# A selective-scan layer with a mixture of experts: products of VectorE moved behind further scans, and the output tiles of one chunk spread over four tiles

## What is computed

```python
proj = xn @ W_in.T                      # x and gate, 1024 channels each
x = silu(conv_b + sum_j conv_w[:, j] * shifted(x, j))     # 4 taps
ts, Bm, Cm = rms parts of x @ W_x.T     # 32, 16 and 16 wide
dt = softplus(ts @ W_dt.T + b_dt)
state = state * exp(dt * A) + (dt * x) * B_t      # per token, 1024 x 16 states
y = sum over the states of state * C_t
s = ((y + x * D) * silu(gate)) @ W_out.T
```

## Time and profile before

| what | us |
|---|---|
| three runs | 1053.42, 1053.86, 1055.64 |
| median | 1053.86 |
| the profiled execution, its own time | 1055.66 |
| its span in the trace | 1053.8 |
| busy: VectorE, GpSimd, TensorE, ScalarE | 986.1, 905.0, 851.3, 727.2 |
| mean granted clock of TensorE, share of full speed | 0.916 |

### The profile page before, as it was taken

How to read it: one execution, slowest core, us unless ns; L and a number is a source line. 1 busy time by engine, 2 the same in 40 slices (tenths; PEclk the granted TensorE clock), 3 DMA queues, 4 the chain that set the end, 5 groups by cost and what they waited for, 6 DMA issues and landing times.

```text
span 1053.8 us, 10364 instructions
## 1 busy us (share of the span) xinstructions
PE 851.3 (81%) x2756; PEld 316.7 (30%) x2756; DVE 986.1 (94%) x1027; ACT 727.2 (69%) x1281; POOL 905.0 (86%) x320
## 2 busy tenths in 40 slices
PE   9944558989878998999756759999888998779468
PEld 6321113333323343333212213333323333223123
DVE  6779999999999999999999899999999988999996
ACT  3656766888877767888565566878778576667543
POOL 0616899979989998989898979799998988999996
PEclk9976669999989999999877879999999999889788
DMA  9947659887778577676843743966648566664735
GB/s 337 348 154 305 229 193 330 289 296 272 267 265 334 180 256 268 241 264 216 272 130 132 217 194 121 332 240 216 219 172 301 187 214 236 228 230 170 279 51 149
DMA packets 86585, 245.93 MB, mean 233 GB/s; under 512 B 9344, under 2 KB 10752, under 8 KB 79872
## 3 DMA queue, kind: packets, MB, share of 16 engines
q1 hardware_dynamic: 67712, 197.03, 52.3%
q10 hardware_dynamic: 12672, 31.46, 7.6%
q0 software_dynamic: 6144, 16.78, 6.1%
HBM read 183.11 MB, written 62.13 MB: 233 GB/s over the span
## 4 chain that ended last, share of the span: by engine, by line
POOL 27%; PE 24%; DVE 18%; issue 11%; DMA 10%; ACT 7%; SPq 2%; ACTq 0%; DVEq 0%; POOLq 0%
POOL drive L593 16%; DVE sc_ps L1197 7%; POOL drive L606 6%; PE x_ps L1519 5%; DMA rep<-rep_rows 5%; PE f_ps L1472 4%; DMA rep_rows<-dtu 3%; DVE drive L1197 3%; PE dt_ps L1447 3%; DVE drive L1207 3%; PE y_ps L1487 3%; ACT sc_ps L806 2%; PE x_ps L1383 2%; POOL slot_x L557 2%; POOL moe L578 2%
## 5 line engine op out<-in xcount | busy, mean ns | idle before, releaser
L593 POOL TENSOR_TENSOR drive<-rep,b_all 128x2048 f32<-128x2048 f32 x127 | 579.0, 4598 | 46.8 <-DMA rep<-rep_rows 37.5
L806 ACT ACTIVATE sc_ps<-rep,a_neg 128x512 f32<-128x512 f32 x512 | 331.2, 681 | 93.7 <-DVE drive L1207 68.1
L1487 PE MATMUL y_ps<-drive,stack 128*32 128x512 f32 x1024 | 152.2, 669 | 108.6 <-DVE drive L1207 68.1
L606 POOL TENSOR_TENSOR drive<-drive,c_all 128x1024 f32<-128x1024 f32 x92 | 219.7, 2388 | 10.1 <-ACT state L785 10.0
L1197 DVE TENSOR_TENSOR_SCAN sc_ps<-sc_ps,state,drive 128x512 f32<-128x512 f32 x164 | 202.4, 1272 | 2.1 <-POOL drive L593 1.4
L1207 DVE TENSOR_TENSOR drive<-sc_ps,c_all 128x1024 f32<-128x1024 f32 x164 | 199.8, 1219 | 3.5
L1197 DVE TENSOR_TENSOR_SCAN sc_ps<-sc_ps,drive 128x512 f32<-128x512 f32 x164 | 193.4, 1214 | 9.2 <-ACT sc_ps L806 5.2
L1472 PE MATMUL f_ps<-w_ring,xT_slot 128*128 128x512 f32 x368 | 172.8, 613 | 23.5 <-ACT xT_slot L816 22.4
L1447 PE MATMUL dt_ps<-xnT,w_g 128*128 128x512 f32 x232 | 120.5, 667 | 23.5 <-ACT dtu L773 23.5
L1197 DVE TENSOR_TENSOR_SCAN drive<-sc_ps,state,drive 128x512 f32<-128x512 f32 x92 | 113.8, 1268 | 7.7 <-ACT sc_ps L806 7.7
L1197 DVE TENSOR_TENSOR_SCAN drive<-sc_ps,drive 128x512 f32<-128x512 f32 x92 | 109.8, 1210 | 3.1 <-ACT sc_ps L806 2.0
(11 more groups left out here) (189 smaller groups left out, 1057.5 us busy)
## 6 DMA issues: line engine op xcount, KB each, us to landing
rep<-rep_rows SPq DMA_DIRECT2D x128, 512.0 KB, 6.1
w_ring<-wring SPq DMA_DIRECT2D x46, 1024.0 KB, 6.1
rep_rows<-dtu ACTq DMA_DIRECT2D x32, 512.0 KB, 2.7
x_slot<-slot_x SPq DMA_DIRECT2D x46, 256.0 KB, 7.0
slot_rows<-y_slot ACTq DMA_DIRECT2D x46, 256.0 KB, 4.3
w_g<-wg_in SPq DMA_DIRECT2D x32, 256.0 KB, 7.4
w_x<-wx_in SPq DMA_DIRECT2D x24, 256.0 KB, 5.2
slot_x<-zeros SPq DMA_DIRECT2D x1, 5888.0 KB, 20.5
```

Of the source, the lines that this page charges most:

```text
L593: pool.tensor_tensor(drive[:, m % RING, :, :], rep[:, n % 2, :, 1, :], b_all[:, q:q + 1, :].broadcast_to([P, NR, TC]), ALU.mult).then_inc( ...
L606: pool.tensor_tensor(drive[:, m % RING, 0:2, :], drive[:, m % RING, 0:2, :], c_all[:, q:q + 1, :].broadcast_to([P, 2, TC]), ALU.mult).then ...
L806: act.activation(sc[:, r, :], rep[:, n % 2, r, 0, :], ACT.Exp, scale=a_neg[:, lo:lo + 1]).then_inc(decay_ok, 1)
L1487: last = pe.matmul(y_ps[CH * r:CH * (r + 1), :], stack[:, :], drive[:, m % RING, r, :], start=False, stop=(m % NQ == NQ - 1))
```

## The change

Four things are changed; every computation stays the same.

- The low product, where VectorE has it, moves from behind scan 1 to behind scan 2 in quads 0, 2 and 3 of every tile (in quad 1, and in quad 3 of the last tile, it stays).
- In the tiles of `SILU_SOON`, the first scan of quad 2 moves ahead of the high product of quad 1, and the first scan of quad 3 ahead of the high product of quad 2.
- `SILU_SOON` loses tiles 0.7, 1.0, 1.1 and 2.7, and so holds 3.0 to 3.6.
- The output tiles of chunk 2 are spread over 3.0 to 3.3, one each, all in halves; for chunk 0 the split stays as it was. The second half goes behind the step sizes' matmul, its copy on ScalarE behind the softplus, and the copy of a whole output tile (chunk 0 only) behind the store of dt and u and `decays(m + 1, 0)`.

```diff
--- before.py
+++ after.py
@@ -52,7 +52,7 @@
 EARLY_X = {3: 1, 4: 3, 5: 5, 6: 7}
 STEPS_AMONG_SCANS = (1, 3, 5, 10, 15, 19, 21, 26, 27, 29)
 GATE_BEHIND = (3, 5, 9, 10, 15, 18, 19, 21, 25, 26, 27, 29, 30)
-SILU_SOON = (7, 8, 9, 23, 24, 25, 26, 27, 28, 29, 30)
+SILU_SOON = (24, 25, 26, 27, 28, 29, 30)
 LATE_X = {2: 0, 3: 2, 4: 4, 5: 6}
 
 
@@ -82,6 +82,18 @@
 
 def late_x(c, t):
     return LATE_X.get(t) if c < NCH - 1 else None
+
+
+def split_out(c, t):
+    if c % PER_ROW == 0:
+        return None
+    if c == NCH - 1:
+        return t if t < TT else None
+    return 2 * t if t < TT // 2 else None
+
+
+def whole_out(c, t):
+    return 2 * t + 1 if c % PER_ROW and c < NCH - 1 and t < TT // 2 else None
 
 
 def pool_pairs(m):
@@ -926,15 +938,14 @@
                 elif t < NT - 1:
                     keep_dt(n + 1)
                 copy_slot_y(b, left_slot)
-                if not even and t in (1, 2):
-                    copy_out(c - 1, 2 * t - 1)
                 diagonal(n)
                 if t < NT - 1:
                     keep_rows(n + 1)
                 store_slot(b, left_slot)
-                if not even and t in (1, 2):
-                    store_out(c - 1, 2 * t - 1)
                 decays(m + 1, 0)
+                if t and whole_out(c, t - 1) is not None:
+                    copy_out(c - 1, whole_out(c, t - 1))
+                    store_out(c - 1, whole_out(c, t - 1))
                 if chunk_end:
                     keep_dt(n + 1)
                     keep_rows(n + 1)
@@ -971,14 +982,13 @@
                 if rms_tile:
                     rms(c + 1)
                 decays(m + 3, 1)
-                if not even and t in (0, 1):
-                    copy_out(c - 1, 2 * t)
-                if not even and t in (0, 1):
-                    store_out(c - 1, 2 * t)
                 if rms_tile:
                     rms_root(c + 1)
                 elif n + 2 < TILES:
                     softplus(n + 2)
+                if split_out(c, t) is not None:
+                    copy_out(c - 1, split_out(c, t))
+                    store_out(c - 1, split_out(c, t))
                 if n == 0:
                     scale_rows(5, RT)
                 if n in TAKES:
@@ -1269,8 +1279,8 @@
                     scan(m, 1)
                     if pe_log(n + 1):
                         times_x(n + 1)
+                    scan(m, 2)
                     low_product(m)
-                    scan(m, 2)
                     scan(m, 3)
                     if chunk_end and not pe_log(n + 1):
                         step_sizes(n + 1)
@@ -1293,19 +1303,19 @@
                 scan(m + 1, 3)
                 if after_odd and t == 2:
                     out_tile(c - 1, 3)
-                if early is not None:
+                if early is not None or n in SILU_SOON:
                     scan(m + 2, 0)
                 products(m + 1, 1)
 
-                if early is None:
+                if early is None and n not in SILU_SOON:
                     scan(m + 2, 0)
                 scan(m + 2, 1)
-                low_product(m + 2)
                 if after_odd and t == 1:
                     out_tile(c - 1, 0)
                 scan(m + 2, 2)
+                low_product(m + 2)
                 scan(m + 2, 3)
-                if late is not None:
+                if late is not None or n in SILU_SOON:
                     scan(m + 3, 0)
                 products(m + 2, 1)
                 if after_odd and t == 1:
@@ -1313,13 +1323,16 @@
 
                 if late is not None:
                     tap(NT * (c + 1) + late, 1)
-                else:
+                elif n not in SILU_SOON:
                     scan(m + 3, 0)
                 scan(m + 3, 1)
                 if late is not None:
                     tap(NT * (c + 1) + late, 2)
-                low_product(m + 3)
+                if n == TILES - 1:
+                    low_product(m + 3)
                 scan(m + 3, 2)
+                if n < TILES - 1:
+                    low_product(m + 3)
                 if late is not None:
                     tap(NT * (c + 1) + late, 3)
                 if n in STEPS_AMONG_SCANS:
@@ -1578,19 +1591,19 @@
                         add_ssm(c + 1, s)
                 if c and even and t == 0:
                     out_tile(c - 1, 0)
-                if not even and t in (0, 1):
-                    out_tile(c - 1, 2 * t, 0, HK)
+                if split_out(c, t) is not None:
+                    out_tile(c - 1, split_out(c, t), 0, HK)
                 if late is not None:
                     next_x(NT * (c + 1) + late)
                 turn_slot(b, second_slot)
                 sums(m + 1)
-                if not even and t in (0, 1):
-                    out_tile(c - 1, 2 * t, HK, NT)
                 if rms_tile:
                     pe.wait_ge(g_ok, n + 1)
                     means_of(c + 1)
                 elif n + 2 < TILES:
                     step_sizes(n + 2)
+                if split_out(c, t) is not None:
+                    out_tile(c - 1, split_out(c, t), HK, NT)
                 if c and even and t == 0:
                     out_tile(c - 1, 1)
                 expert(b, second_slot)
@@ -1599,8 +1612,8 @@
                     out_tile(c, 2, t - 1, t)
                     out_tile(c, 1, 0, t)
                 sums(m + 2)
-                if not even and t in (0, 1):
-                    out_tile(c - 1, 2 * t + 1)
+                if whole_out(c, t) is not None:
+                    out_tile(c - 1, whole_out(c, t))
                 if c and even and t == 1:
                     out_tile(c - 1, 2)
                     out_tile(c - 1, 3, 0, HK)
```

## The result

The changed kernel takes 1060.31 us (median of 14 runs, 1057.16 to 1063.17) against 1054.57 for the kernel before (14 runs): a ratio of 1.0046, 95% interval 1.0035 to 1.0058. By the ratio that is 4.9 us slower where the prediction had 2.7 us faster, and outside its range; the two medians by themselves stand further apart, 5.7 us or 1.0054, since the ratio is not their quotient. The profiled execution took 1061.99 us, span 1060.1, against 1055.66 and 1053.8.

The account below looks back on a forecast made before the run. No single engine was taken as the bound; VectorE, GpSimd, TensorE and ScalarE share the chain. Tiles 3.0 to 3.6 gave -2.8 us, the rest +0.1, so -2.7: median 1053.86 to 1051.2, range 1047.0 to 1055.8.

Parts of the forecast that it names:

- The step that failed: Chunk 3: the store of dt and u in 3.1 goes out about 6 us earlier, removing GpSimd's two replica waits, 8.2 us.
- The second step: Chunk 2's output tiles: 7.1 us of TensorE moves from 3.0 to 3.2, another from 3.1 to 3.3, outside the chain.
- slower: the slot's transpose: Tiles 3.1 to 3.5: a later TensorE transpose delays ScalarE's chain, five tiles by 1.0 us, 1056.2 in all; chance 0.17.
- Tile 3.6: Tile 3.6 takes 1.9 us less, if GpSimd's gathers, waiting for the last slot's store, arrive about 2.3 us earlier.
- The price of the first scans ahead: Tiles 3.0 to 3.6: scans ahead of high products leave VectorE idle, 12.4 us new less 1.6 saved.
- the ledger: Time change per tile, 3.0 to 3.6: -0.9, -3.8, -1.6, +1.3, +1.3, +2.8, -1.9; sum -2.8 us.
- The six idles before quad 2's first scan: VectorE idles there in 3.0 to 3.5: 0.6 us where the gate is behind, 1.2 where ahead, 3.4 in 3.5.
- The softplus idles: VectorE idles 1.4 us before the first softplus step in 3.2, 3.3 and 3.5, and 0.65 in 3.4.
- Tile 2.1: In its quad 2, VectorE idles 1.2 us before scan 2 and the product ends 1.05 later: +1.0 us.
- The low products: Moved off their own scans in 27 quads, each saving 0.115 us on VectorE.
- +0.1 for the rest: Outside 3.0 to 3.6: +1.0 in 2.1, -0.6 in 2.7, small low product savings elsewhere; together +0.1 us.
- GpSimd's rival: GpSimd alone sets the end, so all 8.2 us of its waits come out, giving 1045.9; chance 0.13.

Follow-up runs that it names:

- f: Changed kernel with the 1 MB expert's weight load of tile 3.0 issued behind the replicas of tile 3.2; ratio 1.0011 to the kernel before.
- k: j with only quad 2's first scan put ahead of quad 1's high product again in 3.0 to 3.6; ratio 0.9984 to the kernel before.
- e: Changed kernel with TensorE's gate matmuls of tile 3.2 put ahead of the last sums of 3.1; ratio 1.0016 to the kernel before.
- a: Changed kernel with the first scans of quads 2 and 3 back behind the high products in 3.0 to 3.6; ratio 0.9938 to the kernel before.
- h: f with ScalarE's SiLU and table loads behind quad 2's first pair of decays in 3.0 to 3.6; ratio 0.9927 to the kernel before.
- l: j with only quad 3's first scan put ahead of quad 2's high product again in 3.0 to 3.6; ratio 0.9927 to the kernel before.
- j: a with the expert's weight load of tile 3.0 issued behind the replicas of tile 3.2; ratio 0.9934 to the kernel before.
- d: Kernel before with only the low products of quads 0, 2 and 3 moved behind the third scan; ratio 1.0001 to the kernel before.
- c: Kernel before with only the output tiles of chunks 2 and 0 and their copies in their new places; ratio 0.9952 to the kernel before.

## Why the prediction was wrong

**The step that failed** is this one: "The store took 12.7 us to become a drive's release ...; issued at 837.4 it gives 850.1 ... So both GpSimd waits go: 8.2 us." The issue time was right (837.57), the 12.7 was not: it measured 19.0. It had been taken where the DMA engines were 0.10 busy, and was moved to a place where a 1 MB load had just been issued. The store landed in 8.2 instead of 2.7 us, and GpSimd's waits came to 8.3 us as before. So tile 3.1 gave 2.0 us and not 3.8. Moving the load away (f) brought 3.7 us, and the 3.8 of tile 3.1.

**The second step** that failed costed the output tile at nothing on TensorE: "7.1 us of TensorE moves from 3.0 to 3.2 and another from 3.1 to 3.3, where it is not in the chain." In 3.1 it was a burden, as forecast: without it the sums of 3.2 start 4.8 us earlier. But it was cover too: it kept TensorE busy while GpSimd's product was late, and so kept its clock, and of the 4.8 us 3.1 went to the lower clock. Together these two steps make tile 3.2 cost +4.3 instead of -1.6; with the replicas in time (f) it costs 0.0. The trace before had the same event one tile on, in 3.3, with gate matmuls of 4.50 us behind it:

```profile
900.76 1.94 PE L1487 MATMUL y_ps<-drive,stack 128*32 128x512 f32 x8 [5.72 <-POOL drive L606]
```

I used only its last link, the 0.80 of the earlier trace rows.

**The rival "slower: the slot's transpose"** is what happened, with a chance of 0.17: the transpose late, the ScalarE chain slid, the scan passed it on. It had five tiles by 1.0 us; it was one tile by 4.8 (5.44 less the 0.6 forecast). Its cause was not the half tiles on the queue but GpSimd's late product and the gap where a whole tile had been.

**Tile 3.6**, forecast at -1.9 "if GpSimd's gathers allow it", gave +0.4. The gather waited 4.3 us for the last slot's store (issued 988.90, gather 995.67, 6.8 us), and VectorE then 2.55 for the drive. The store moved with VectorE's losses of 3.3 to 3.5 and not with GpSimd's pace. In k, e and f the gather waits 5.5, 5.3 and 3.5; in a and h, which don't carry those losses, nothing but the issue. This was my condition and I took its good side.

**What held.** The price of the first scans ahead: 8.1 to 10.8 us by the tile sums, 8.5 and 11.4 measured. In 3.3, 3.4 and 3.5 the ledger was right to 0.2 us. The six idles before quad 2's first scan were right except in 3.2. The softplus idles stand as forecast (1.35 three times), but their price is in doubt: l has them and is no slower than j. Tile 2.1 has its 1.14 us at scan 2, 3.7 its 1.15.

**The low products.** Of the 3.1 us that 27 freed products would save, the forecast books only 0.6 (0.3 in 3.0 to 3.6, the rest elsewhere), against 1.0 lost in 2.1; its +0.1 for the rest holds 0.6 us for the SiLU of 2.7 besides. d measured 1.0001 within 0.12%. That is compatible with these sums, and doesn't tell them from nothing saved. In the rows, though, a product with another scan in front starts ahead of that scan's end: in 3.1, 848.80+1.28=850.08 against 850.00. As in the earlier trace rows, independent neighbours overlap. The section of the Trainium skill that the prediction names there (VectorE: DVE Perf Modes, The DRAIN you can't avoid) goes on to say that a next instruction that is not held starts earlier, so these rows don't stand against the skill, as the prediction has it.

**Sum.** Of the 7.6 us between forecast and result by the ratio (9.1 by the medians), f gives back 3.7 (5.4). What is left lies, in f's row of the ledger, in 3.2 (1.6 us above the forecast), 3.4 (1.6) and 3.6 (1.5), against 1.1 gained in 3.0. In 3.4 TensorE stands 3.62 us for the copy of a slot's result and its next sums take 1.94; it was not taken apart further. The sum for GpSimd's rival has a slip: 1053.86 less 8.2 is 1045.7, not 1045.9, and nothing hangs on it.

## What to carry to other kernels

Before booking an earlier DMA, look at what its queue and the shared DMA engines carry in the stretch that it moves to, and never carry over a landing time from an idle stretch. Matmuls that look like dead weight ahead of a wait may be what keeps TensorE at its higher clock until the wait ends; ask what fills the gap when they go. And two orders that are each free (the SiLU ahead of the decays, the next scan ahead of the product) can together cost 0.8 to 1% (f against h and j), since each used the slack that hid the other.

## What the runs showed of the hardware

TensorE's clock has two levels in the rows, 1.2 and 2.4 GHz: the sums' eight matmuls take 1.94 or 1.06 us, the gate's eight 3.70 at the higher and up to 5.89 where most of them fall into the slow stretch. It fell in gaps of 3.65 us (e), 4.45 (c) and 5.72 (after). In f, where this was not expected and the one wait is of 1.77 us, it was still 1.00 when the sums began at 864.77 and fell only once the matmuls ran again: 1.00 from 865 to 866, 0.50 from 867 to 869. In c, e, f and after it came back during the gate's matmuls. Runs of one kernel spread by some 6 us here (1057.16 to 1063.17 for the change), much for differences of 0.2%. Issued 0.2 to 1.1 us behind a 1 MB load, a store of 512 KB landed in 6.8 to 8.2 us, and in 2.7 to 4.8 otherwise; why 2.7 in some of these and 4.8 in others is open. Whether the stalls of 3.2 stand in some executions and not in others, which would explain a's and j's medians, stays open: each kernel was profiled once.
